# Moving small vector work, a residual add and a store between the queues of a two-layer graph kernel

## What is computed

```python
h = relu(layernorm(x));  x = x + (A @ (h @ W + b)) / deg[:, None]
X = relu(layernorm(x));  S = S + eye
Rf, Rb = S / S.sum(1)[:, None], S / S.sum(0)[:, None]
Xf = Xb = Xa = X;  Z = 0
for s in range(2):
    logits = Xa @ W1 @ W2 @ (Xa @ W3).T
    # keep, row by row, the largest softmax entries until their sum passes 0.9
    A = softmax(where(in_the_nucleus(logits, 0.9), logits, -inf))
    Xf, Xb, Xa = Rf @ Xf, Rb @ Xb, A @ Xa
    Z = Z + Xf @ U1[s] + Xb @ U2[s] + Xa @ U3[s]
x = x + layernorm(X + Z) * gamma + beta
```

## Time and profile before

| | us |
|---|---|
| median of 3 runs | 2281.59 (2280.49 to 2283.03) |
| the profiled execution | 2276.97 |
| its span, first to last instruction | 2275.3 |
| PE busy | 1915.2 (84%) |
| DVE busy | 1710.6 (75%) |
| ACT busy | 1232.0 (54%) |
| POOL busy | 84.9 (4%) |
| chain that ended last | PE 45%, DVE 31% |

### The profile page before, as it was taken

How to read it: one execution, slowest core, us unless ns; L and a number is a source line. 1 busy time by engine, 2 the same in 40 slices (tenths; PEclk the granted TensorE clock), 3 DMA queues, 4 the chain that set the end, 5 groups by cost and what they waited for, 6 DMA issues and landing times.

```text
span 2275.3 us, 38276 instructions
## 1 busy us (share of the span) xinstructions
PE 1915.2 (84%) x12364; PEld 1432.6 (63%) x12364; DVE 1710.6 (75%) x4468; ACT 1232.0 (54%) x1922; POOL 84.9 (4%) x141
## 2 busy tenths in 40 slices
PE   4999944899999999995855499999989999999980
PEld 3999922677777777774753356566665656566660
DVE  4222255888888888888861888888889888888957
ACT  4222245566666666663613667576666767575620
POOL 3000020000000000000000000000000000000000
PEclk9999967899999999997978699999999999999995
DMA  6888620111111111110103010101101010101103
GB/s 159 181 177 173 159 82 27 39 43 43 43 43 43 43 43 43 43 43 21 41 6 98 19 38 18 37 18 37 33 22 37 18 37 18 37 18 37 32 6 124
DMA packets 59325, 123.91 MB, mean 54 GB/s; under 512 B 13587, under 2 KB 45713, under 8 KB 59024
## 3 DMA queue, kind: packets, MB, share of 16 engines
q1 hardware_dynamic: 45968, 93.58, 12.0%
q0 software_dynamic: 3744, 22.14, 6.3%
q10 hardware_dynamic: 9568, 7.67, 1.1%
HBM read 107.99 MB, written 37.49 MB: 64 GB/s over the span
## 4 chain that ended last, share of the span: by engine, by line
PE 45%; DVE 31%; DVEq 12%; issue 6%; ACT 3%; DMA 1%; SPq 0%; ACTq 0%; POOL 0%; POOLq 0%
PE bank L903 13%; PE bank L880 6%; DVE stats L1280 5%; PE bank L894 5%; DVE window L1150 5%; PE lg L860 4%; DVE scraps L1150 4%; PE bank L805 4%; PE lg L805 3%; DVEq L1455 3%; PE bank L926 3%; DVEq L1327 2%; DVE window L1323 2%; PE bank L786 2%; DVE sorted_e L1289 1%
## 5 line engine op out<-in xcount | busy, mean ns | idle before, releaser
L903 PE MATMUL bank<-xcur,probs_t 128*128 128x256 f32 x2704 | 597.4, 381 | 37.9 <-ACT probs_t L702 37.9
L903 PEld LDWEIGHTS bank<-xcur,probs_t 128*128 128x128 f32 x2704 | 509.5, 190 | 117.5 <-ACT probs_t L702 47.0
L702 ACT ACTIVATE probs_t<-bank 128x512 f32<-128x512 f32 (+1 forms) x364 | 190.5, 565 | 308.9 <-PE bank L894 308.8
L894 PE MATMUL bank<-ident,window 128*128 128x128 f32 x1352 | 207.7, 297 | 150.7 <-DVE kept_inv L1457 138.6
L894 PEld LDWEIGHTS bank<-ident,window 128*128 128x128 f32 x1352 | 156.2, 149 | 252.8 <-DVE kept_inv L1457 162.4
L880 PE MATMUL bank<-both,s_tile 128*128 128x512 f16 x1352 | 300.1, 379 | 0.0
L1135 DVE TENSOR_SCALAR_CACHE_REDUCE expo<-lg 128x1024 f32 (+1 forms) x208 | 204.9, 1022 | 80.3 <-PE lg L860 63.3
L668 ACT ACTIVATE turned<-expo,found 128x3327 uint8<-128x3327 f32 x78 | 239.6, 3072 | 5.4
L649 ACT ACTIVATE expo<-expo,neg_max 128x3327 f32<-128x3327 f32 x52 | 159.7, 3070 | 152.6 <-DVE neg_max L1144 152.4
L666 ACT ACTIVATE turned<-expo,found 128x3327 uint8<-128x3327 f32 x78 | 239.3, 3068 | 3.8 <-issue 0.2
L860 PE MATMUL lg<-k_t,q_tile 64*128 64x512 f32 (+1 forms) x832 | 201.3, 584 | 44.7 <-DMA q_tile<-q_scratch 23.3
(11 more groups left out here) (246 smaller groups left out, 2196.3 us busy)
## 6 DMA issues: line engine op xcount, KB each, us to landing
s_tile<-s_scratch SPq DMA_DIRECT2D x52, 832.0 KB, 4.6
expo<-in_adj POOLq DMA_DIRECT2D x25, 831.8 KB, 9.1
s_scratch<-s_tile SPq DMA_DIRECT2D x14, 832.0 KB, 9.0
s_scratch<-probs_t SPq DMA_DIRECT2D x6, 832.0 KB, 9.2
s_scratch<-window SPq DMA_DIRECT2D x6, 832.0 KB, 9.0
x_scratch<-both SPq DMA_DIRECT2D x1, 3328.0 KB, 9.5
q_tile<-q_scratch SPq DMA_DIRECT2D x104, 32.0 KB, 3.2
xa_scratch<-ht ACTq DMA_DIRECT2D x26, 128.0 KB, 1.7
```

Of the source, the lines that this page charges most:

```text
L702: A.activation(probs_t[:, k0 * P:(k0 + n) * P], flip_ps[g % 2][:, 0:n * P], ACT.Copy).then_inc(p_moved[s], 1)
L894: last = T.transpose(flip_ps[g % 2][:, k * P:(k + 1) * P], window[:, (k0 + k) * P:(k0 + k + 1) * P], ident[:, :])
L903: last = T.matmul(pv_ps[:, 0:D], probs_t[:, k * P:(k + 1) * P], xcur[:, k, :], start=(k == 0), stop=(k == NT - 1))
```

## The change

Five edits, sent together:

1. First step: PE no longer adds the features to y with a product by the identity (line 920). Instead ACT leaves y in `y_tile`, POOL adds the features to it (`x_added`), and the store of y goes from ACT's queue to SP's, where it stands in the loop body behind the load of the adjacency and waits for `x_added` of tile t.
2. Both steps: the product of the probabilities no longer waits for all seven groups at its start. Only the last two groups are waited for, each ahead of its own blocks. (The first five are covered by the waits of the transposes.)
3. Second step: the late logits come after groups 1 and 3, not 2 and 4.
4. Second step: POOL makes the bracket from `found` in a second loop, `first_bracket`, of 21 small instructions and 9 drains for a tile, and leaves it in `lead`.
5. Second step: DVE waits for `lead_ready` in place of `expo_ready`, copies `lead`, takes one reciprocal and one combination, and goes on.

```diff
-LATE_AFTER = (2, 4)
+LATE_AFTER = ((2, 4), (1, 3))
...
                     if not is_last(t):
                         load_s(t + 1, m + b, 1 - b)
+                    if s == 0:
+                        sp.wait_ge(x_added, t + 1)
+                        sp.dma_start(dram_tile(y_dram, tile_of(m, b)), y_tile[:, :]).then_inc(y_stored[0], DMA)
                     if s == 1:
                         sp.wait_ge(y_done[1], t + 1)
...
                 G.tensor_tensor(tile4(both, tile_of(m, b), 1), xfb[:, :], tile4(both, tile_of(m, b), 0), ALU.subtract).then_inc(lo_ready[0], 1)
+                pool.wait_ge(y_out[0], t + 2)
+                G.tensor_tensor(y_tile[:, :], y_tile[:, :], tile3(xcur, tile_of(m, b)), ALU.add).then_inc(x_added, 1)
             tiles_loop(pool, low_parts)
...
+            def first_bracket(t, m, b):
+                pool.wait_ge(expo_ready[1], t + 1)
+                ends, whole = lead[:, b, 8:12], found[:, b, 4:5]
+                G.tensor_tensor(aims[:, :], found[:, b, 1:4:2], found[:, b, 6:7].broadcast_to([P, 2]), ALU.add)
+                G.tensor_copy(lead[:, b, 4:7], found[:, b, 4:7])
+                G.tensor_copy(scalar_points[:, 0:4:2], found[:, b, 0:4:2])
+                G.tensor_scalar(ends, ends_t[:, :], whole, None, ALU.mult)
+                G.tensor_scalar(span[:, :], found[:, b, 0:4:2], AIM[1] + GUARD, None, ALU.mult)
+                pool.drain()
+                G.tensor_tensor(ends, ends, ends_c[:, :], ALU.add)
+                G.tensor_tensor(aims[:, :], aims[:, :], span[:, :], ALU.add)
+                pool.drain()
...
+                G.tensor_copy(lead[:, b, 2:3], span[:, 1:2])
+                G.tensor_tensor(lead[:, b, 1:2], span[:, 0:1], lead[:, b, 11:12], ALU.mult).then_inc(lead_ready, 1)
+            tiles_loop(pool, first_bracket)
...
                         A.activation(y_tile[:, :], pv_ps[:, 0:D], ACT.Copy).then_inc(y_out[0], 1)
-                        act.wait_ge(y_out[0], t + 2)
-                        act.dma_start(dram_tile(y_dram, tile_of(m, b)), y_tile[:, :]).then_inc(y_stored[0], DMA)
...
                     pe.wait_ge(y_out[s], t + 1)
-                    pe.wait_ge(p_moved[s], (t + 1) * NG)
-                    for k in range(NT):
-                        last = T.matmul(pv_ps[:, 0:D], probs_t[:, k * P:(k + 1) * P], xcur[:, k, :], start=(k == 0),
-                                        stop=(k == NT - 1))
+                    for g, (k0, n) in enumerate(P_GROUPS):
+                        if g >= NG - 2:
+                            pe.wait_ge(p_moved[s], t * NG + g + 1)
+                        for k in range(k0, k0 + n):
+                            last = T.matmul(pv_ps[:, 0:D], probs_t[:, k * P:(k + 1) * P], xcur[:, k, :], start=(k == 0),
+                                            stop=(k == NT - 1))
...
-                    if s == 0:
-                        T.matmul(pv_ps[:, 0:D], ident[:, :], tile3(xcur, tile_of(m, b)), start=True, stop=False)
-                    else:
+                    if s == 1:
                         pe.wait_ge(y_loaded[1], DMA * (t + 1))
...
-                    dve.wait_ge(expo_ready[s], t + 1)
                     if s == 0:
+                        dve.wait_ge(expo_ready[0], t + 1)
                         V.tensor_copy(cut, found_of(b, 2, 3))
                         V.tensor_copy(mine[:, 4:7], found_of(b, 4, 7))
                     else:
-                        V.tensor_copy(mine[:, 0:7], found_of(b, 0, 7))
+                        dve.wait_ge(lead_ready, t + 1)
+                        V.tensor_copy(mine[:, :], lead_of(b))
                     dve.drain()
                     if s == 1:
-                        bracket_from_scalar()
+                        V.reciprocal(weight[:, :], mine[:, 2:3])
+                        dve.drain()
+                        V.scalar_tensor_tensor(out=cut, in0=weight[:, :], scalar=mine[:, 1:2], in1=bracket[:, 0:1],
+                                               op0=ALU.mult, op1=ALU.add)
                         if not is_last(t):
                             copy_logits(t + 1, other, LOGITS_LATE)
```

More of the change, by code:

```diff
@@ L172, in graph_layers @@
         step_by = acts[:, 6:7]
-        mine = sb("mine", [P, 8])
+        mine = sb("mine", [P, 12])
+        lead = sb("lead", [P, 2, 12])
+        scalar_points = sb("scalar_points", [P, 4])
+        aims = sb("aims", [P, 2])
+        picked = sb("picked", [P, 2, 8])
+        left_out = sb("left_out", [P, 2, 4])
+        span = sb("span", [P, 2])
         points = [mine[:, 2 * r:2 * r + 2] for r in range(2)]
@@ L180, in graph_layers @@
         my_slack = mine[:, 6:7]
[L181 removed]
+        bracket = mine[:, 8:12]
         ends_t = sb("ends_t", [P, 4])
@@ L497, in _ @@
             G.memset(odd[:, :], 0.0)
+            G.memset(lead[:, :, :], 0.0)
             for b in range(2):
@@ L538, in low_parts, with twice, pairs @@
                 G.tensor_tensor(tile4(both, tile_of(m, b), 1), xfb[:, :], tile4(both, tile_of(m, b), 0), ALU.subtract).then_inc(lo_ready[0], 1)
+                pool.wait_ge(y_out[0], t + 2)
+                G.tensor_tensor(y_tile[:, :], y_tile[:, :], tile3(xcur, tile_of(m, b)), ALU.add).then_inc(x_added, 1)
             tiles_loop(pool, low_parts)
+            def twice(two):
+                return two.rearrange("p (a d) -> p a d", a=1).broadcast_to([P, 2, 2])
+            def pairs(four):
+                return four.rearrange("p (a d) -> p a d", a=2)
@@ new lines, in first_bracket @@
+            def first_bracket(t, m, b):
[10 more added lines that the diff above has]
+                pool.drain()
+                G.tensor_scalar(scalar_points[:, 1:4:2], aims[:, :], -1.0, None, ALU.mult)
+                pool.drain()
+                for r in range(2):
+                    G.tensor_scalar(picked[:, r, 0:4], sides[:, :], scalar_points[:, 2 * r + 1:2 * r + 2], 0.0, ALU.mult, ALU.is_gt)
+                    G.tensor_scalar(left_out[:, r, :], sides[:, :], scalar_points[:, 2 * r + 1:2 * r + 2], 0.0, ALU.mult, ALU.is_le)
+                pool.drain()
+                for r in range(2):
+                    G.tensor_tensor(pairs(picked[:, r, 4:8]), pairs(picked[:, r, 0:4]), twice(scalar_points[:, 2 * r:2 * r + 2]), ALU.mult)
+                for r in range(2):
+                    G.tensor_tensor(ends, ends, left_out[:, r, :], ALU.mult)
+                    pool.drain()
+                    G.tensor_tensor(ends, ends, picked[:, r, 4:8], ALU.add)
+                    pool.drain()
+                G.tensor_tensor(span[:, :], lead[:, b, 10:12], lead[:, b, 8:10], ALU.subtract)
+                pool.drain()
+                G.tensor_copy(lead[:, b, 2:3], span[:, 1:2])
+                G.tensor_tensor(lead[:, b, 1:2], span[:, 0:1], lead[:, b, 11:12], ALU.mult).then_inc(lead_ready, 1)
@@ L925, in step @@
                         for c in range(DC):
-                            last = T.matmul(pv_ps[:, 0:D], turned_part[:, c, :], u_sb[:, j, c, :], start=False,
+                            last = T.matmul(pv_ps[:, 0:D], turned_part[:, c, :], u_sb[:, j, c, :], start=(s == 0 and j == 0 and c == 0),
                                             stop=(j == 2 and c == DC - 1))
@@ L1127, in found_of, with lead_of @@
                 return found[:, bass.ds(b, 1), c0:c1].rearrange("p a n -> p (a n)")
+            def lead_of(b):
+                if isinstance(b, int):
+                    return lead[:, b, :]
+                return lead[:, bass.ds(b, 1), :].rearrange("p a n -> p (a n)")
             for s in range(2):
@@ L1169, in interpolate @@
                     dve.drain()
-                def bracket_from_scalar():
-                    V.scalar_tensor_tensor(out=bracket[:, :], in0=ends_t[:, :], scalar=my_total, in1=ends_c[:, :],
-                                           op0=ALU.mult, op1=ALU.add)
-                    V.tensor_scalar(reach[:, :], mine[:, 0:4:2], AIM[1] + GUARD, my_slack, ALU.mult, ALU.add)
-                    dve.drain()
-                    V.scalar_tensor_tensor(out=mine[:, 1:4:2], in0=mine[:, 1:4:2], scalar=-1.0, in1=reach[:, :], op0=ALU.mult,
-                                           op1=ALU.subtract)
-                    dve.drain()
-                    for r in range(2):
-                        V.tensor_scalar(which[:, 4 * r:4 * r + 4], sides[:, :], points[r][:, 1:2], 0.0, ALU.mult, ALU.is_gt)
-                    dve.drain()
-                    for r in range(2):
-                        replace_ends(r)
-                    interpolate()
                 def evaluate(b):
```

9 lines of the change are left out of this document (6 added, 3 removed).

## The result

The changed kernel takes 2398.33 us (2397.65 to 2399.26, 4 runs) against 2281.12 us (2280.49 to 2283.03, 4 runs) before: a ratio of 1.0513 [1.0494, 1.0531], 5% slower. Forecast: 2383, range 2340 to 2450.

The account below looks back on a forecast made before the run. The prediction took PE to bound the first step (29.20 us a tile) and DVE the second (36.58). Its terms, +145 - 46 + 4 - 2 = +101, on the median 2281.59 gave 2383 us, range 2340 to 2450.

Parts of the forecast that it names:

- the term of +5.8 us a tile, +145: First step: SP's store delays the next flags and queries; net of PE's savings +5.8 us a tile, +145 over 25.
- 8.0 both: First step: the queries' way and the flags' way each end 8.0 us after the end of y on PE.
- +0.8 for the clock behind them: First step: transposes and ACT's chain behind a partly slow PE cost +0.8 us a tile, from 0 to 2.2.
- 6.15 + 0.8 = 6.95: First step: transposes start 6.15 us later behind y, plus 0.8 for slow PE, before PE's savings are taken off.
- all 1.18 us of PE as gained: First step: product's wait 0.74 and identity product 0.44 both leave PE's path, 1.18 us of the 29.20 period.
- -1.85 a tile forecast: Second step: moving the bracket to POOL saves DVE a net 1.85 us a tile, -46 us over 25 periods.
- The 2.15: Second step: DVE's stretch from the copy of found to the late logits shrinks from 2.94 to 0.8 us, -2.15.
- the +0.3 for collisions of small instructions: Second step: small DVE instructions that meet POOL's lose 0.3 us a tile.
- POOL should be through just ahead of line 1331: Second step: POOL's 5.8 us chain ends at 1722.2, just ahead of DVE's long two-input instruction.
- my third rival's condition: Second step: POOL held by line 1331 or taking 9 us, so its chain comes late; 2421 us, chance 10%.
- Cost none: Second step: making the late logits earlier costs nothing, since PE has over 2 us in hand.
- +145 - 46 + 4 - 2 = +101: Whole kernel, us: first step +145, second step's bracket -46, its start +4, first and last tile's savings -2.

Follow-up runs that it names:

- experiment 2: The kernel before with only the store of y moved from ACT's queue to SP's, without POOL's addition: 2441.8 us.
- experiment 1: The kernel after with SP's store of y moved one tile later, behind the load of the adjacency: 2217.81 us, 0.9722 of before.
- 3: The kernel after with the store of y back on ACT's queue, waiting there for POOL's addition: 2218.51 us.
- Experiment 5: The kernel after with 20 unread products added on PE in the first step while it waits for the queries: 2399.86 us.
- 7: The kernel of experiment 1 with the product again waiting for all seven groups at its start, in both steps: 2225.39 us.
- 8: The kernel of experiment 1 with the identity product back on PE and no addition on POOL: 2226.64 us.
- Experiment 12: The kernel of experiment 1 with ACT copying the product's result between its two passes, and that result's store issued behind the turned-block copies: 2201.39 us, 0.9656 of before.
- experiment 10: The kernel of experiment 1 with 12 unread small additions and 12 drains more on POOL in the second step: 2261.87 us.
- experiment 9: The kernel of experiment 1 with the second step's late logits back behind groups 2 and 4: 2242.14 us.
- experiment 6: The kernel after with one unread ACT pass of 900 columns more in the first step, ahead of the copy of the product's result: 2433.24 us.
- experiment 4: The kernel after with the next body's queries loaded ahead of SP's store, the flags still behind it: 2368.61 us.

## Why the prediction was right, point by point

**The store in SP's queue: right, and shown.** Alone it makes the kernel before slow (experiment 2); undone, it makes the kernel after faster than before (1, 3). The comparison of two times that carried the prediction, flags at 925.31 against y's end at 930.48, was enough to find it.

**Its size: the term of +5.8 us a tile, +145, was mis-sized.** It measured 6.7 for a regular tile (35.91 - 29.20), +165 over the 25. The traces give it as a sum of other parts than mine. `kept_inv` started 0.6 us ahead of y's end (929.87 and 930.48; 0.5 in every other tile) and starts 8.2 behind it now (5.6 until the flags are read, 2.6 more): +8.7. But DVE used to wait right behind `kept_inv` for PE's early logits, and no longer does: -1.5.

```profile
931.59 1.22 DVE L1135 TENSOR_SCALAR_CACHE_REDUCE expo<-lg 128x1024 f32 x1 [1.55 <-PE lg L860]
```

From `ht` to the end of y PE takes 4.9 us for 5.5: -0.5. Sum +6.7. Against it two steps of the prediction were wrong.

- I gave PE's path (queries, early logits at half clock, transposes) and DVE's (flags, `kept_inv`) as equal, 8.0 both, and then added +0.8 for the clock behind them. Experiment 5 takes the slow logits out and gains nothing. The true ring does not pass through them. That 6.15 + 0.8 = 6.95 comes so near to the measured 8.7 - 1.5 = 7.2 is luck: the 0.8 happened to stand for a `kept_inv` that ends 8.3 us behind y in the mean and not 7.85, and for what this does to DVE and not to PE.
- I counted all 1.18 us of PE as gained, since PE sets the period and DVE has over 2 us in hand. This is the larger part of the error, 0.65 us a tile. With the store out of the way, only 29.20 - 28.67 = 0.53 is gained (experiment 1). DVE's time in hand at one place said nothing on a second ring, logits to ACT's passes to `ht` to PE, that is 28.67 long without the identity. In it the identity counts in full, 0.43, and the product's wait for 0.10 of its 0.74 (7, 8), together the 0.53. Experiment 12 gets 1.29 out, once `ht` and its copies are early.

The pieces behind the y that ends at 972.62: ACT 0.42 forecast, 0.41 measured; POOL to 1.2, to 1.32; the store at SP 1.49 behind y; queries 1.9 forecast, 2.5 measured, since the next issue came 1.0 behind the store's and not 0.7 (it is 0.67 in every other tile); flags 3.1 forecast, 3.7 measured; landing 2.0, 2.03; `kept_inv` 7.85 forecast, 8.46 measured. The half clock was right for the logits (3.3 forecast, 3.79 measured).

**Edits 4 and 5: right.** -1.85 a tile forecast, -2.2 measured. The 2.15 is exact; the +0.3 for collisions of small instructions was not needed. "POOL should be through just ahead of line 1331" was nearly so: the first 19 of its 21 instructions took 5.4 us (5.8 forecast for all), the next copy fell under the long instruction and took 3.41; for the same reason POOL is busy for 7.5 us a tile and not some 4. The Trainium skill says in "GPSIMD Engine Reference", section 8, that POOL contends with DVE instructions that have two SBUF inputs. This 3.41 us agrees, and it was my third rival's condition: POOL does stand still there. What decides is that 2.45 us are left behind it; experiment 10 shows the other side of that point.

**Edit 3: the step that was too easy.** "Cost none" was right (PE still waits 0.7 to 0.9 us for `kept_inv`), but it is worth 1.0 us a tile beside edit 4 (experiment 9), some 25 us: without it the second step would give back half its gain. I had seen the clock fall in 8 of 23 stretches, and held it for a matter of some tenths. I had also read PE's time in hand from one row of 2.26 us; in 8 of the 24 periods, those behind a slow one, PE waits only 0.65 to 1.14 for `kept_inv`.

**Start of the second step:** +4 forecast, +4.5 measured. **The tail:** not forecast, +2.9. A loop of 26 DVE instructions at the very end, before (line 1487) and after (line 1531, a part):

```profile
2230.80 9.80 DVE L1487 TENSOR_SCALAR parts<-parts,mean,rstd  x26 [0.39 <-issue]
```

```profile
2350.06 0.73 DVE L1531 TENSOR_SCALAR parts<-parts,mean,rstd  x2 [0.31 <-issue]
```

The same instructions, with a gap of some 0.3 us ahead of nearly each pair. Experiment 1 has it too, experiment 2, whose DVE program is that of before, has not. Why is open; no run tries it.

**Sum.** Forecast +145 - 46 + 4 - 2 = +101; measured +165.2 - 51.9 + 4.5 + 2.9 = +120.7, the difference of the spans. By the spans I was 20 us low, as much as the first step's term was (165.2 for 145); the other terms cancel. Against the medians it is 15 us, since the profiled execution of the kernel before was 4 us shorter than its median.

## What to carry to other kernels

A DMA queue is a program in order: before a wait is put into it, compare the time at which the wait ends with the time at which the next instructions of that queue leave today. Had that store been placed one tile later, the same change would have given 0.972 instead of 1.051. Where an engine has time in hand, follow every ring through it before counting a saving in full, and where two paths are less than one us apart don't trust the profile's chain: lengthen or shorten one of them and look at the period.

## What the runs showed of the hardware

- POOL stood still until a long DVE instruction with two inputs had ended, even for a copy of one column: 3.41 or 3.51 us in place of some 0.2, in 23 tiles of the kernel after; in experiment 10 up to 3.68, the length of the DVE instruction. The small POOL instruction that started together with it, at 1867.26, took its usual 0.20.
- PE was still at half its clock behind idle stretches much shorter than the 5.3 us of the kernel after: in experiment 9 in 7 of 22 periods, with waits for `kept_inv` of 1.43 to 1.58, in experiment 6 behind 1.90 to 2.31. In the kernel after, from 1500 to 2200, where the wait is 0.69 to 0.86, the clock is at 1.00. Which period of experiment 9 is hit can't be told from its wait: the slow and the fast ones have the same. In the kernel before 8 of 16 waits of 2.1 to 2.3 us were followed by it.
- On SP the queries were issued 0.67 or 1.0 us behind the instruction ahead of them by turns, with the two halves of the loop body: 0.67 and 0.99 behind the store in the kernel after, 0.63 and 0.99 in experiment 1, 0.68 and 0.96 behind the adjacency's load in the kernel before. The flags came 0.41 and 0.84 behind the store by turns in experiment 4. I have no reason for it.
